# Layer-0 attention in groups of four heads: scores and weighted sums back to back, probabilities turned in the bank of their scores

## What is computed

```python
xn = (x - mu) * jax.lax.rsqrt(var + LN_EPS) * gamma
q = (xn @ w_q).reshape(b, n, HEADS, DIM_HEAD)          # 16 heads of 64
k, v = jnp.split(xn @ w_kv, 2, axis=-1)                # two null keys and values go in front
q = _l2norm(q) * q_scale
k = _l2norm(k) * k_scale
sim = jnp.einsum('bhid,bhjd->bhij', q, k) * ATTN_SCALE
sim = sim + dist[None, None] * slopes[None, :, None, None]
sim = jnp.where(causal_mask[None, None], neg, sim)
attn = jax.nn.softmax(sim, axis=-1)
out = jnp.einsum('bhij,bhjd->bhid', attn, v)
return out.transpose(0, 2, 1, 3).reshape(b, n, HEADS * DIM_HEAD) @ w_out
```

## Time and profile before

| | |
|---|---|
| time, median of 3 runs | 1047.17 us (1043.44 to 1049.5) |
| span of the profiled execution | 1043.3 us |
| busy, share of the span | PE 92%, PEld 66%, DVE 66%, ACT 60%, POOL 62% |
| granted PE clock, mean | 0.986 of full speed |
| PE busy in step 9 (476.44 to 517.68 us) | 40.81 of 41.24 us |
| step 0 to layer 0's experts | to 312 us |
| layer 0's experts | 312 to 397 us |
| step 6 to the end of step 15 | 397 to 795 us |

### The profile page before, as it was taken

The page is one execution under the profiler, slowest core; times in us unless marked ns, Lnnn a source line. Parts: engine busy times, 40 slices in busy tenths (PEclk is TensorE's granted clock), DMA queues, the critical chain, the costliest instruction groups (busy, mean ns, idle before and its releaser), DMA issues.

```text
span 1043.3 us, 21426 instructions
## 1 busy us (share of the span) xinstructions
PE 961.4 (92%) x6330; PEld 690.3 (66%) x6330; DVE 692.3 (66%) x2589; ACT 630.9 (60%) x1945; POOL 650.4 (62%) x803
## 2 busy tenths in 40 slices
PE   5699989999999979999999999999998999999965
PEld 2465546666658976666665665666666788999954
DVE  6988867886673335867768768677885474345634
ACT  4458857667664557677676775766765564444442
POOL 4663787888855544667776678788746651555540
PEclk9889999999999999999999999999999999999997
DMA  9300202202427783033032030331232134787759
GB/s 296 79 7 6 42 27 66 71 26 64 113 74 188 221 233 84 10 72 81 6 66 50 22 71 26 73 67 41 52 82 52 34 102 143 227 229 226 219 168 242
DMA packets 95444, 103.19 MB, mean 99 GB/s; under 512 B 10096, under 2 KB 83031, under 8 KB 95089
## 3 DMA queue, kind: packets, MB, share of 16 engines
q1 hardware_dynamic: 88752, 89.36, 33.5%
q0 software_dynamic: 6592, 12.65, 3.5%
HBM read 77.54 MB, written 23.50 MB: 97 GB/s over the span
## 4 chain that ended last, share of the span: by engine, by line
PE 54%; DVE 18%; ACT 7%; POOL 7%; issue 6%; DMA 3%; SPq 3%; DVEq 0%; POOLq 0%; ACTq 0%
PE bank L1347 9%; PE bank L823 8%; PE bank L834 7%; PE bank L1376 7%; PE bank L1403 5%; DVE arena L2032 5%; PE bank L1391 4%; ACT arena L1759 4%; PE bank L1366 3%; PE bank L1426 3%; DVE arena L2041 3%; POOL arena L1130 2%; DVE arena L1932 2%; POOL expert_rows L655 2%; DMA arena<-in_b 1%
## 5 line engine op out<-in xcount | busy, mean ns | idle before, releaser
L1759 ACT ACTIVATE arena<-arena 128x128 f32<-128x128 f32 (+1 forms) x512 | 226.9, 446 | 96.7 <-DVE arena L2032 96.5
L2032 DVE CUSTOM_DVE_ANT_0 arena<-bank,arena 128x128 f32<-128x128 f32 (+1 forms) x512 | 183.0, 412 | 107.1 <-PE bank L1376 104.4
L1347 PE MATMUL bank<-arena 128*128 128x512 f32 x384 | 211.1, 636 | 6.0 <-ACT arena L1748 3.6
L1130 POOL TENSOR_TENSOR arena<-arena 128x512 f32<-128x512 f32 x128 | 133.4, 1045 | 121.7 <-ACT arena L1735 104.1
L2041 DVE COPY arena<-bank 128x384 f32<-128x384 f32 x256 | 130.0, 549 | 21.1 <-PE bank L1391 20.9
L1145 POOL TENSOR_TENSOR arena<-arena 128x512 f32<-128x512 f32 x128 | 129.5, 1048 | 1.3
L1735 ACT ACTIVATE arena<-bank 128x512 f32<-128x512 f32 x192 | 112.7, 588 | 27.8 <-PE bank L1347 27.5
L1391 PEld LDWEIGHTS bank<-const,arena 128*128 128x128 f32 x768 | 91.3, 142 | 56.0 <-issue 55.0
L784 POOL DMA_INDIRECT expert_out<-arena x71 | 71.1, 1002 | 90.0 <-DVE arena L923 42.1
L1376 PE MATMUL bank<-arena 64*128 64x128 f32 (+1 forms) x1024 | 119.3, 351 | 2.2 <-DVE arena L2032 1.5
L1403 PE MATMUL bank<-arena 128*64 128x256 f32 (+1 forms) x1024 | 112.2, 340 | 9.1 <-DVE arena L2041 8.7
(11 more groups left out here) (304 smaller groups left out, 1634.1 us busy)
## 6 DMA issues: line engine op xcount, KB each, us to landing
arena<-in_wp SPq DMA_DIRECT2D x40, 514.0 KB
arena<-recip_rows SPq DMA_DIRECT2D x30, 512.0 KB, 6.4
XN<-in_wp SPq DMA_DIRECT2D x24, 514.0 KB
arena<-expert_rows SPq DMA_DIRECT2D x46, 129.0 KB, 3.2
arena<-in_b SPq DMA_DIRECT2D x64, 64.0 KB
arena<-expert_out SPq DMA_DIRECT2D x16, 256.0 KB, 5.1
expert_out<-fill SPq DMA_DIRECT2D x11, 338.6 KB, 7.9
expert_rows<-fill SPq DMA_DIRECT2D x1, 2644.5 KB, 21.6
```

The source lines that it names most:

```text
L1130: pool.tensor_tensor(sq[:, i % 2], r, r, ALU.mult).then_inc(S["sq_done"], 1)
L1347: mm = pe.matmul(RING[bnk][:, :], xa[:, p, t * P:(t + 1) * P], wqkv[:, 512 * k:512 * k + 512], start=True, stop=True)
L1759: ins = act.activation(w, w, ACT.Exp, bias=nm[:, p, 16 * t + h:16 * t + h + 1], scale=-1.0, accum_out=den[:, p, 16 * t + h:16 * t + h + 1])
L2032: ins = v.tensor_tensor_reduce(out=SPb[:, c % 2, 384 * k + P * t:384 * k + P * t + n], in0=SBANK[k][:, P * t:P * t + n], in1=alibi[:, h, N ...
```

## The change

Two pairs are one group d (`NFOUR` = 4 groups in a step). The two pairs of a group have two banks each, `PAIRBANK = (SBANK, TBANK)`. On PE a group is now: first ring part, transposes of pair 2d, second ring part, transposes of pair 2d + 1, third ring part, scores of the next two pairs, weighted sums of this group's two pairs. The transposes of a head go to the bank that held its scores, so that the scores of pair c + 2 wait until DVE has copied out the turned probabilities of pair c. DVE and ACT follow the same order. `RING_USES` has three parts for each of four groups, in the same sequence as before. `denominators` moves from the end of a step to its successor's first pair, `comb_out` from pair 0 to pair 1, `seeds` from pair 6 to pair 7, and the `sums` are spread a little later. What is computed by each instruction is the same.

```diff
 RING_USES = {
-    0: ([("unit", 8, 1)], [("unit", 10, 1)]),
-    1: ([("qk", 0, 1), ("qk", 1, 1)], [("unit", 0, 2), ("qk", 2, 1)]),
...
+    0: ([("unit", 8, 1)], [("unit", 10, 1), ("qk", 0, 1)], [("qk", 1, 1), ("unit", 0, 2), ("qk", 2, 1)]),
+    1: ([("qk", 3, 1)], [("unit", 1, 2), ("qk", 4, 1)], [("unit", 2, 2), ("qk", 5, 1), ("unit", 3, 2), ("qk", 6, 1)]),
+    2: ([("unit", 4, 2)], [("qk", 7, 1), ("unit", 5, 2)], [("unit", 6, 2), ("unit", 7, 2)]),
+    3: ([("unit", 9, 1)], [("unit", 11, 1)], [])}
+NFOUR = NPAIR // 2
...
+        PAIRBANK = (SBANK, TBANK)
...
-                        mm = pe.matmul(SBANK[k][:, P * t:P * t + n], qT[r:r + 64, p, c, t * P:(t + 1) * P],
+                        mm = pe.matmul(PAIRBANK[c % 2][k][:, P * t:P * t + n], qT[r:r + 64, p, c, t * P:(t + 1) * P],
...
-                    if not isinstance(b, int) or b or c:
-                        pe.wait_ge(S["pt_evac"], b * 16 + (2 * c + k - 1))
                     for j in range(3):
-                        mm = pe.transpose(TBANK[k][:, P * j:P * j + P],
+                        mm = pe.transpose(PAIRBANK[c % 2][k][:, P * j:P * j + P],
...
-                for c in range(NPAIR):
-                    if c + 1 < NPAIR:
-                        pe.wait_ge(S["ttr_done"], b * 16 + (2 * c + 2))
-                        scores(p, c + 1)
...
+                for d in range(NFOUR):
+                    ring(d, 0)
+                    turn_p(b, 2 * d)
+                    behind_turns(2 * d)
+                    ring(d, 1)
...
+                    turn_p(b, 2 * d + 1)
+                    behind_turns(2 * d + 1)
+                    ring(d, 2)
...
+                    if d + 1 < NFOUR:
+                        for c in (2 * d + 2, 2 * d + 3):
+                            pe.wait_ge(S["pt_evac"], b * 16 + (2 * c - 2))
+                            scores(p, c)
+                    elif more:
+                        pe.wait_ge(S["ring_evac"], ring_use(b, ("qk", NQ - 1, 1)) + 1)
+                        for c in range(2):
+                            pe.wait_ge(S["pt_evac"], b * 16 + (2 * c + 14))
+                            scores(1 - p, c)
...
+                    for c in (2 * d, 2 * d + 1):
+                        weigh(b, p, c)
...
-            pe.wait_ge(S["ttr_done"], (FB + 1) * 16 + 2)
+            pe.wait_ge(S["ttr_done"], (FB + 1) * 16 + 4)
             ffn_tensor(pe, 0, NBLK0, 0, loads0)
...
+                for d in range(NFOUR):
+                    c = 2 * d
+                    probs(b, p, c, 0)
+                    probs(b, p, c, 1)
+                    probs(b, p, c + 1, 0)
+                    ring(d, 0)
+                    probs(b, p, c + 1, 1)
+                    if d:
+                        out_evac(b, p, d - 1)
...
+                    ring(d, 1)
...
+                    ring(d, 2)
...
                     if c == 0 and before and not flushed:
+                        denominators(b - 1, 1 - p)
+                    if c == 1 and before and not flushed:
                         comb_out(b - 1)
...
-                    if c == 6 and more == 2:
+                    if c == 7 and more == 2:
                         seeds(b + 2)
...
+            SUMS = {2: (0,), 3: (1,), 4: (2, 3), 5: (4,), 6: (5, 6), 7: (7,)}
...
+            denominators(FB, FB % 2)
             comb_out(FB)
```

122 lines of the change are left out of this document (48 added, 74 removed), and 2 rows, old and new, of the table RING_USES.

## The result

The changed kernel takes 1067.03 us (median of 4 runs, 1060.84 to 1070.94), the kernel before 1047.64 us (4 runs, 1043.44 to 1049.5). The prediction was 1041 us, a small gain, with a range of 1020 to 1058: it has the wrong sign, and it is 26 us short. The profiled execution took 1070.94 us, its span is 1069.1 us against 1043.3 before.

The account below looks back on a forecast made before the run. PE was taken to bound the attention steps. Ordinary steps -2.0, step 1 -4.5, steps 10 and 12 -5.5, experts +2.1, last step +3.6 gave -6.3 us; with the span's difference to the median, 1041 us, range 1020 to 1058.

Parts of the forecast that it names:

- second rival: The new order leaves PE without new waits and the full 2.1 us a step stay: 1018 us, chance 0.17.
- Part 1: PE's scores and sums: two pairs share three changes of matmul shape, saving about 0.53 us a group, 2.1 a step.
- Part 2: Each group walked through PE, DVE and ACT: new waits in groups 0 and 1 take 1.8 us; an ordinary step gains 0.2.
- Part 3: Moved work: `denominators`, 1.36 us of DVE, is covered by the wait for pair 1's transposes; later `turn_comb` and `comb_out` cost nothing.
- Part 4: Late steps: steps 10 and 12 gain 5.5 us together as `denominators` moves, step 1 gains 4.5.
- third rival: POOL, not DVE's order, makes steps 1, 10 and 12 long, so their 10 us don't come: 1051 us, chance 0.13.
- Part 5: Seams: into the experts +3.1 us, behind them -1.0, together +2.1; the last step +3.6 to 30.1 us.
- The chain in every group: Rival: each group waits 0.4 us more than walked, a step costs +1.6; about 1058 us, chance 0.25.
- The clock: Rival: waits behind the experts and the thin last step lower PE's clock, some 2 us each: 1045 us; chance 0.05 with unforeseen waits.

Follow-up runs that it names:

- e2: Changed kernel with `denominators` put ahead of pair 0's copies on DVE instead of behind them; ratio to the kernel before 1.0084.
- e8: e7 with DVE's sums of squares that stood ahead of the copies of pairs 2, 4 and 6 moved behind these; ratio to the kernel before 1.0070.
- e9: e7 with only the sums of squares of slots 2 and 3 moved behind the copies of pair 4; ratio to the kernel before 0.9976.
- e7: e6 with ACT emptying the second part's ring banks ahead of the sums' bank `OB`; 1043.66 us, ratio to the kernel before 0.9985.
- e10: e9 with DVE computing `denominators` at the end of step 5 before the next two pairs' maxima, ahead of the experts; ratio to the kernel before 0.9957.
- e12: Changed kernel with POOL's eight 512-column multiplications of the normalisation replaced by memsets; one run only, no ratio, step 4 took 38.88 us.
- the control: The changed kernel itself, run again unchanged on another chip; 1070.57 us, ratio to the kernel before 1.0240.
- e6: e2 with `qk` 0 moved from group 0's second ring part to the start of its third; 1048.63 us, ratio to the kernel before 1.0035.
- e3: Changed kernel with `seeds` back at pair 6, and the last sums of squares as in the kernel before; ratio to the kernel before 1.0269.

## Why the prediction was wrong

The prediction's sum was 6.3 us below the kernel before, so a span of 1037; it was 1069.1 in the profiled execution. The 32.1 us, by its own terms (distances between the same marks in both timelines):

| term | predicted | measured | off by |
|---|---|---|---|
| ordinary steps 2 to 4, 7 to 9, 11, 13 | -1.6 | +6.1 | 7.7 |
| step 14, counted as ordinary | -0.2 | +3.1 | 3.3 |
| steps 1, 10, 12 | -10.0 | +5.1 | 15.1 |
| step 5, into, through and behind the experts | +1.9 | +6.9 | 5.0 |
| up to step 1 (-3.4), last step (+4.7), behind it (+3.3) | +3.6 | +4.6 | 1.0 |

Two sums in the prediction are slightly off: 1.51 + 1.45 is 2.96 us, not 2.98 (2.96 is also what was measured), and the second rival comes to 1041 - 25 = 1016 us, not 1018. Neither matters for what follows.

**Part 1, the shape of matmuls: right.** Second scores and second sums at 0.65 us (two pairs' less the first pair's), groups 2 and 3 shorter by 0.55 each (11.44 to 10.89, 8.47 to 7.92), where 0.53 was worked out.

**Part 2, the walk: right for groups 2 and 3, 0.2 short for group 1 in the early steps, wrong for group 0.** Groups 2 and 3 are 10.89 and 7.92 us where the walk had 10.8 and 7.9; group 1 is 10.34 for 10.1 in step 4. The walk was made for this kind of step only: in step 8, where layer 1's gate products (`lg`) stand in the ring too, group 1 is 11.65 for 10.71 before, and PE waits twice for ACT's emptying there, 0.25 us each. `qk` 0 waits 1.1 us for 1.0, with POOL's multiplication as releaser. Group 0 failed: 11.4 for 9.9. Of the 1.5 us, 1.07 went with the wait at `turn_comb` (e2); 0.4 stays: `qk` 0 starts 6.7 us into the group in e2 (227.33 to 234.04) and not 6.5, and what follows takes 3.6 us and not 3.4.

**Part 3, "covered, costs nothing": this step failed, and it made an ordinary step 0.9 to 1.1 us longer (e2 against the changed kernel).** With it mended the steps are 0.1 to 0.2 us longer than before (39.49 for 39.30, 41.34 for 41.24), where the sum had them 0.2 shorter. Two errors are in it. The duration of `denominators` was taken from where it stood, and not asked for where it goes: beside POOL's 512-column pieces it takes 3.1 us and not 1.36. And the one who waits was looked for at POOL's scaling and `project`, some 20 us into the step, when `turn_comb` itself waits on PE's queue, with all of PE's work behind it. The trace of before had the warning: its median for L2058 is 0.19 us, but its longest is 1.08, as this row shows (minimum, median, maximum in ns).

```profile
L2058 DVE TENSOR_TENSOR arena<-arena x32: 176/192/1082, 105.6 to 794.2; 128x32 f32<-128x32 f32 x32
```

Five of those 32 are over 0.5 us, all of them beside L1145. An operation's median over a run is the price beside its old neighbours. The Trainium skill has the rule (SBUF — State Buffer, section Who interferes with whom): a DVE instruction with two SBUF inputs contends with a GpSimd instruction that reads SBUF, not with one that only writes it, and the loser fully blocks. The traces agree with it on each point: 0.58 to 1.08 us beside L1143, each time up to the end of one of POOL's multiplications, 0.19 beside the memset, and the one-input reduction unchanged. The prediction weighed no rule on DVE at all.

**Part 4, the late steps: the largest term, 15.1 of the 32.1 us.** Step 1 took 49.6 us (the prediction 43, the kernel before 47.3), step 12 took 47.9 (42.6; 45.3), step 10 took 44.2 (41.3; 44.0). The 2.75 us at the end of step 1 did go: its groups take 15.10, 12.08, 14.47 and 7.91 us, against 11.45, 10.37, 11.57 and 13.90 before. But the first three lost more, by the waits for POOL and DVE in group 0, by waits of 1.17 and 0.33 us for ACT in group 2, and by the clock. That the late steps stay late was the third rival, with a chance of 0.13, and its outcome came. Its reason, POOL and not DVE's order, holds in half. In group 2 of step 12 both act: DVE waits 2.64 us for a square of POOL, and since this sum stands ahead of the copy and of the null scores (L2013), PE waits 2.65 us with it.

```profile
689.91 0.69 DVE L1932 TENSOR_REDUCE arena<-arena 128x8 f32<-128x512 f32 x1 [2.64 <-POOL arena L1128]
690.51 1.01 DVE L2041 COPY arena<-bank 128x384 f32<-128x384 f32 x2
```

Moved behind them (e8, e9) the wait is gone, so the order mattered; in group 3, 2.3 us come back, so it was not all. Step 1 takes 44.5 us in e7 and 46.3 in e10, and it goes with the clock: their groups 2 take 12.89 us at a granted clock of 1.00 and 14.51 at 0.88.

**Part 5, the seams.** Into the experts the walk was exact: 6.08 us from the last scores to the experts (312.31 to 318.39), 6.1 predicted, and DVE's denominators start 3.84 us behind these scores as walked. PE's rows there:

```profile
317.50 0.38 PE L1412 MATMUL bank<-const,arena 128*48 128x128 f32 x2 [2.16 <-DVE arena L2058]
318.39 0.90 PE L813 MATMUL bank<-const,arena 128*128 128x128 f32 x3 [0.51 <-DVE arena L2065]
```

Behind the experts 0.5 us were lost instead of 1.0 won. The experts themselves took 2.3 us longer (87.26 for 84.94), though nothing in them was changed: behind the wait of 2.16 us PE's granted clock in their first 8 us is 0.61, in the kernel before 1.00.

```profile
312.14:320.14 8.00, 7.50 (x45) 6.63 (x46) 2.92 (x8) 3.56 (x9) 6.75 (x7) 1.00 0.66 133
...
318.39:326.39 8.00, 7.38 (x25) 5.88 (x26) 2.65 (x6) 1.65 (x5) 7.33 (x8) 0.61 0.70 139
```

PE's rows count 25 instructions there instead of 45. It is so in every profiled kernel with the new order but e10 and e12: in these two the clock stays at 1.00 there and the experts take 85.65 and 84.36 us, in the others 86.55 to 88.30. The last step took 31.1 us for 30.1.

**The rivals.** *The chain in every group* was the nearest in time (1058), but not in mechanism: no wait came in groups 2 and 3 of the ordinary steps. *The clock* was given 4 us, behind the experts and in the last step. Behind the experts it fell (0.96 over step 6, 38.86 us, against 1.00 and 37.74 in the control); in the last step it did not (1.00). It fell in six other stretches that the prediction hadn't named (step 1 twice, step 3, the experts, steps 12 and 14), and cost about 9 us in this execution: see below.

## What to carry to other kernels

When a step moves to another place in an engine's order, take its duration from where it will run: ask which engines work there, and look at the longest of its durations in the old trace, not at the median. Where two waits stand in a row on one engine, removing one hands its time to the other; here the pair of them (e2 and then e6) gave 1.6 us a step, and the second alone (e3) a loss. Ask who waits first for the moved step's result, not who needs it in the end. And before a difference between two runs is put down to an edit or to scatter, put the granted clock of the stretch beside its time.
